# An EdgeConv layer with a segment maximum on one core: final rows from three stretches, the minimum trees behind the second list, and every final addition on VectorE

## The reference, cut to what matters

```python
h = jnp.maximum(_layernorm(x, axis=-1), 0.0)
x_i, x_j = h[dst], h[src]
feat = jnp.concatenate([x_i, x_j - x_i], axis=-1)
msg = feat @ W.T + b                      # W is 128 x 256
out = jax.ops.segment_max(msg, dst, num_segments=6250)
return x + jnp.where(jnp.isfinite(out), out, 0.0)
```

## Time and profile before

| what | value |
|---|---|
| median of 3 runs | 991.62 us (990.52 to 994.15) |
| the profiled execution, its own time | 995.42 us |
| its span | 993.8 us |
| mean granted clock of TensorE | 0.825 of full |
| busy: TensorE / VectorE / ScalarE / GpSimd | 57% / 85% / 58% / 72% |
| DMA | 182.11 MB, mean 183 GB/s |

### The profile page before, as it was taken

How to read it: one execution, slowest core, us unless ns; L and a number is a source line. 1 busy time by engine, 2 the same in 40 slices (tenths; PEclk the granted TensorE clock), 3 DMA queues, 4 the chain that set the end, 5 groups by cost and what they waited for, 6 DMA issues and landing times.

```text
span 993.8 us, 7917 instructions
## 1 busy us (share of the span) xinstructions
PE 564.1 (57%) x2393; PEld 265.1 (27%) x2393; DVE 846.5 (85%) x1237; ACT 577.9 (58%) x255; POOL 713.8 (72%) x644
## 2 busy tenths in 40 slices
PE   2556970000002366766776676788878888676560
PEld 2443640000001122322222232333333333222240
DVE  7899899987785598999989999899999999758573
ACT  3775113000038999597996987496797976844000
POOL 1587878888875677677767676676777677777745
PEclk9898995555555779888878987999999999988875
DMA  8831222212146466656657776998988778754344
GB/s 256 194 97 21 70 71 79 67 50 77 55 145 217 142 208 223 197 174 222 179 170 232 255 253 201 295 296 300 338 302 321 278 239 259 227 186 139 73 79 148
DMA packets 62901, 182.11 MB, mean 183 GB/s; under 512 B 20358, under 2 KB 33140, under 8 KB 56315
## 3 DMA queue, kind: packets, MB, share of 16 engines
q1 hardware_dynamic: 42530, 140.13, 40.7%
q0 software_dynamic: 20144, 40.52, 17.1%
q10 hardware_dynamic: 184, 0.96, 0.3%
HBM read 127.34 MB, written 55.04 MB: 184 GB/s over the span
## 4 chain that ended last, share of the span: by engine, by line
POOL 29%; DVE 26%; issue 19%; DMA 13%; PE 8%; ACT 3%; POOLq 0%; DVEq 0%; SPq 0%; PEldq 0%
POOL rows L669 22%; DVE acc L1191 10%; DMA rows<-near_table,idx 8%; PE ps L787 8%; DVE maxima L1134 5%; POOL ohs L641 4%; POOL hT L648 3%; DVE hT L1141 3%; DMA running_max<-maxima 2%; DVE pos L878 2%; DVE hT L1154 1%; DVE ohs L1179 1%; DMA ohs<-in_dst,begin_i 1%; DMA ohs<-winners 1%; DVE hT L1146 1%
## 5 line engine op out<-in xcount | busy, mean ns | idle before, releaser
L669 POOL DMA_INDIRECT rows<-near_table,idx x527 | 600.3, 1139 | 206.0 <-issue 138.8
L787 PE MATMUL ps<-ohs,near 128*128 128x481 bf16 x1443 | 351.9, 401 | 142.6 <-DVE acc L1191 119.7
L1191 DVE TENSOR_TENSOR acc<-ps,acc 128x1924 f32<-128x1924 f32 x192 | 336.5, 1779 | 21.8 <-PE ps L787 21.6
L1134 DVE SCALAR_TENSOR_TENSOR maxima<-maxima,fresh,rows 128x128 f32<-128x128 f32 x527 | 185.6, 352 | 72.6 <-DMA rows<-near_table,idx 56.2
L787 PEld LDWEIGHTS ps<-ohs,near 128*128 128x128 bf16 x1443 | 143.7, 105 | 350.1 <-DVE acc L1191 125.8
L548 ACT ACTIVATE ohs<-ohs,neg_l 128x6272 bf16<-128x6272 bf16 x25 | 137.9, 5518 | 123.4 <-DMA ohs<-winners 123.4
L541 ACT ACTIVATE hT<-k,off 128x2400 bf16<-128x2400 int16 x49 | 108.9, 2281 | 131.7 <-DVE hT L1146 115.6
L550 ACT ACTIVATE ohs<-ohs 128x6272 bf16<-128x6272 bf16 x25 | 135.8, 5431 | 0.8
L787 PE MATMUL ps<-sorts_mem,near 128*128 128x481 bf16 x468 | 107.8, 385 | 32.7 <-DVE acc L1191 28.6
L773 PE MATMUL ps<-flags,ones 128*128 128x8 f32 x2 | 0.6, 356 | 173.0 <-DVE spare L1167 173.0
L641 POOL DMA_INDIRECT ohs<-src_pad,start_i x49 | 55.0, 1122 | 34.9 <-DVE start_i L891 20.5
(11 more groups left out here) (173 smaller groups left out, 517.4 us busy)
## 6 DMA issues: line engine op xcount, KB each, us to landing
ohs<-winners SPq DMA_DIRECT2D x37, 1568.0 KB, 7.7
running_max<-maxima SPq DMA_DIRECT2D x90, 512.0 KB, 5.1
sorts_mem<-winners SPq DMA_DIRECT2D x12, 1568.0 KB, 8.0
rows<-near_table,idx POOLq DMA_INDIRECT x527
acc<-in_x SPq DMA_DIRECT2D x6, 512.0 KB, 8.2
near_table<-acc SPq DMA_DIRECT2D x12, 256.0 KB, 4.5
base<-in_x SPq DMA_DIRECT2D x1, 2744.0 KB
out_x<-hT SPq DMA_DIRECT2D x12, 224.0 KB
```

What stands on the lines that cost most here:

```text
L669: nc.gpsimd.indirect_dma_start(rows[:, n % (SLOTS * GATHERS), :], None, near_table[:, :], bass.IndirectOffsetOnAxis(idx[:, n:n + 1], 0)).t ...
L787: last = nc.tensor.matmul(bank(4 * (n % 2) + c - UNITS[r][0])[:, 0:CHUNK], near[:, t, part, :], oh[t % OHS][:, at:at + CHUNK], start=part ...
L1134: V.scalar_tensor_tensor(run_at(n + 1), run_at(n), fresh[:, n:n + 1], rows[:, n % (SLOTS * GATHERS), :], ALU.add, ALU.max).then_inc(chain, 1)
L1191: V.tensor_tensor(into, found, into, ALU.max).then_inc(max_done, 1)
```

## The change

Four things change.

1. **Three tables for the final rows** in place of two. HOMES lists (first j, end of j, first step, end of steps): nodes with j below 36 read steps 0 to 415, j from 36 to 43 read steps 232 to 503, j from 44 to 48 read steps 296 to 527. A block of 8 steps is stored in every table whose range holds it, and block 0 in all. That makes 52 + 35 + 30 = 117 stores; the 15 blocks of steps 296 to 415 are stored three times. Groups 9 and 10 (j 36 to 43) are gathered when block 62 is stored, groups 11 and 12 when all is. Five short VectorE instructions more compute the flags and ends (columns 6 to 9 of flags in place of 6 and 7).
2. **The planner's costs.** A gather costs 1.45 us in the checks and the sort, 2.0 us from the words on and 1.28 us in the rounds; each of the nine early groups of finals costs four gathers more; the third round of every fourth tile costs 3.65 us, since VectorE's one-hot stands there.
3. **All additions on VectorE.** L692 and the semaphore final_added are gone; SyncE waits for final_ready alone.
4. **All trees behind the second list.** Trees 0 to 5 stand one after another behind the list and the verdict, ahead of the first dense round; the rest as before. ScalarE's and SyncE's orders follow the same rules as before: load(0) and load(1) stand behind tree 1, distances of batch 4 behind one_hot(0), those of batch 5 behind one_hot(1).

The planner's answer, worked through with both sets of costs, places the chain's steps as follows (steps placed up to and with that piece of VectorE's work):

| behind | before | after |
|---|---|---|
| the third check | 4 | 8 |
| the tile numbers | 28 | 40 |
| the first half of the last stage of compact | 104 | 108 |
| the second list | 112 | 112 |
| tree 1 | 96 | 116 |
| tree 3 | 108 | 120 |
| tree 5, ahead of the first round | 116 | 124 |
| tile 1 (counted from 1) | 120 | 132 |
| tile 10 | 204 | 240 |
| tile 20 | 296 | 360 |
| tile 30 | 376 | 448 |
| tile 40 | 452 | 496 |
| tile 46 | 500 | 528 |
| tile 49 | 524 | 528 |
| behind all rounds | 528 | 528 |

The diff, cut to its core:

```diff
-CUT, CUT_CAP, CUT_LOW = 36, 416, 232
+HOMES = ((0, 36, 0, 416), (36, 44, 232, 504), (44, 49, 296, 528))
+EARLY = HOMES[0][1] // GROUP
...
     for i in range(stages(1)):
         pieces += [("move", 3.8), ("move", 2.7)]
-        if i >= stages(1) - EARLY_TREES:
-            pieces += tree_pieces(trees)
-            trees += 1
     pieces += [("list", 4.0), ("verdict", 3.0)]
...
     for t in range(49):
-        pieces += [("round", 1.85)] * 4
+        pieces += [("round", 1.85)] * 2 + [("round", 3.65 if t % 4 == 0 else 1.85)] + [("round", 1.85)]
...
+    phase, gather = "lists", {"lists": 1.45, "words": 2.0, "round": 1.28}
+    ending = [FINALS_FROM + g * FINALS_EVERY for g in range(EARLY)]
...
+        if name in gather:
+            phase = name
...
-                issue += GATHERS * (1.3 if name == "round" else 1.85)
+                issue += GATHERS * gather[phase]
                 landed += [issue + 3.0] * GATHERS
+                if n + GATHERS in ending:
+                    issue += GATHERS * gather[phase]
...
-    kept = (CUT_CAP, STEPS + CT - CUT_LOW)
+    kept = [cap - low + STEPS * (low > 0) for _, _, low, cap in HOMES]
...
         def homes(i):
 
             n = i * STEPS
-            return [(0, n)] * (n < CUT_CAP) + [(1, 0)] * (n == 0) + [(1, n - CUT_LOW + STEPS)] * (n >= CUT_LOW)
+            return [(h, n - low + STEPS * (low > 0) if n else 0) for h, (_, _, low, cap) in enumerate(HOMES)
+                    if n == 0 or low <= n < cap]
...
             for g, (a, z) in enumerate(spans):
-                if by_pool(g):
-                    sp.wait_ge(final_added, g // 2 + 1)
-                else:
-                    sp.wait_ge(final_ready, g + 1 - min(g // 2 + 1, groups // 2))
+                sp.wait_ge(final_ready, g + 1)
...
             pool.sem_inc(decided, 1)
-            stored(all_blocks)
-            for g in range(early_groups, groups):
+            for g in range(EARLY, groups):
+                for home in HOMES[1:]:
+                    if spans[g][0] == home[0]:
+                        stored(home[3] // STEPS)
                 finals(g)
-            for g, (a, z) in enumerate(spans):
-                if by_pool(g):
-                    pool.wait_ge(joined, g + 1)
-                    nc.gpsimd.tensor_tensor(rowsF[:, a:z, :], rowsF[:, a:z, :], base[:, a:z, :], ALU.add).then_inc(final_added, 1)
...
-                if not by_pool(g):
-                    dve.wait_ge(joined, g + 1)
-                    V.tensor_tensor(rowsF[:, a:z, :], rowsF[:, a:z, :], base[:, a:z, :], ALU.add).then_inc(final_ready, 1)
+                dve.wait_ge(joined, g + 1)
+                V.tensor_tensor(rowsF[:, a:z, :], rowsF[:, a:z, :], base[:, a:z, :], ALU.add).then_inc(final_ready, 1)
```

More of the change, by code:

```diff
@@ L132, in edgeconv @@
     CT = sum(c for _, _, c in PARTS)
-    early_groups = CUT // GROUP
     spans = [(a, min(a + GROUP, tiles)) for a in range(0, tiles, GROUP)]
@@ L141, in edgeconv @@
     first_blocks, all_blocks = first_steps // STEPS, all_steps // STEPS
-    assert D == P and tiles == 49 and rest and 0 < lastj <= CUT and lastp == P - 1
+    assert D == P and tiles == 49 and rest and 0 < lastj <= HOMES[0][1] and lastp == P - 1
     assert chk_p * chk_w == edges and (4 * P - 1) * hop < edges and UNITS[-1][1] * CHUNK >= nodes
     near_table = nc.dram_tensor("near_table", (tiles * P, D), F32, kind="Internal").ap()
-    kept = (CUT_CAP, STEPS + CT - CUT_LOW)
+    kept = [cap - low + STEPS * (low > 0) for _, _, low, cap in HOMES]
     running = [nc.dram_tensor(f"running_max{h}", (P * c, D), F32, kind="Internal").ap() for h, c in enumerate(kept)]
@@ L217, in edgeconv @@
         end_row = sb("end_row", [P, tiles], I32)
-        flags = sb("flags", [P, 8], F32)
-        flag_s = sb("flag_s", [P, 8], F32)
+        flags = sb("flags", [P, 10], F32)
+        flag_s = sb("flag_s", [P, 10], F32)
         disorder = sb("disorder", [P, 1], I32)
@@ L267, in edgeconv @@
         count_ps = bank(7)[:, 256:257]
-        flag_ps = bank(3)[:, 0:8]
+        flag_ps = bank(3)[:, 0:10]
         x_pad_set = sem("x_pad_set")
@@ L333, in edgeconv @@
         final_ready = sem("final_ready")
-        final_added = sem("final_added")
         out_done = sem("out_done")
@@ L344, in by_dve @@
             return t % 4 == 3
-        def by_pool(g):
-            return g % 2 == 0 and g < groups - 1
         def act_count(t):
@@ L646, in finals @@
                 for j in range(a, z):
-                    h = 0 if j < CUT else 1
+                    h = sum(j >= end for _, end, _, _ in HOMES)
                     nc.gpsimd.indirect_dma_start(
@@ L671, in _ @@
                             bass.IndirectOffsetOnAxis(idx[:, n:n + 1], 0)).then_inc(gathered[b % SLOTS], 16)
-                for g in range(early_groups):
+                for g in range(EARLY):
                     if (b + 1) * GATHERS == FINALS_FROM + g * FINALS_EVERY:
@@ L675, in _ @@
                             pool.wait_ge(m_ready, len(batches))
-                            stored(CUT_CAP // STEPS)
+                            stored(HOMES[0][3] // STEPS)
                         finals(g)
@@ L1048, in loser_words @@
                 if h:
[L1049 to L1054, removed]
+                    for i, (begin, end, low, most_steps) in enumerate(HOMES):
+                        of = slice(max(begin, a), end)
+                        if end < z:
+                            then(V.tensor_scalar(flags[:, 6 + i:7 + i], tot[:, end - a:end - a + 1],
+                                                 float(most_steps - first - 1), None, ALU.is_gt))
+                        if low:
+                            then(V.tensor_scalar(flags[0:lastp, 7 + i:8 + i],
+                                                 tot[0:lastp, begin - a:begin - a + 1], float(low - first), None, ALU.is_lt))
+                        then(V.tensor_scalar(end_f[:, of], tot[:, of.start - a + 1:end - a + 1], float(first),
+                                             float(most_steps - 1), ALU.add, ALU.min))
                     settled()
-                    then(V.tensor_scalar(end_f[:, CUT:z], end_f[:, CUT:z], float(STEPS - CUT_LOW), 0.0, ALU.add, ALU.max))
+                    for begin, end, low, _ in HOMES[1:]:
+                        then(V.tensor_scalar(end_f[:, begin:end], end_f[:, begin:end], float(STEPS - low), 0.0, ALU.add, ALU.max))
                 else:
@@ L1064, in loser_words @@
                 settled()
-                for at, end, rows_kept in ((a, CUT, kept[0]), (CUT, z, kept[1])) if h else ((a, z, kept[0]),):
+                for at, end, rows_kept in ([(max(u[0], a), u[1], r) for u, r in zip(HOMES, kept)] if h else [(a, z, kept[0])]):
                     then(V.scalar_tensor_tensor(end_row[:, at:end], part_f[:, 0:1].to_broadcast([P, end - at]),
```

## The result

The changed kernel takes 1009.1 us (median of 4 runs, 1003.2 to 1017.0) where the kernel before takes 992.5 us: ratio 1.0168, 95% interval 1.013 to 1.0205. It is slower, where 981.5 us and a gain were forecast. Its profiled execution took 1005.5 us with a span of 1003.8, so 10.0 us more than the span before; this execution lies 0.4% under its kernel's median and the profiled one of before (995.4 us) 0.3% over its own, which is why the medians stand further apart.

What follows compares the result with a forecast made beforehand. Bounds: GpSimd before the second list, VectorE in the rounds, a chain of single steps at the end. Start 364 + rounds 598.8 + end 21.0 = 983.8 us against 993.8, so 981.5 us beside the median; range 957 to 1002.

Steps and rivals of the forecast that it cites:

- The end: Behind the last round: final rows gathered beside rounds, serial VectorE work left, 21.0 us in place of 40.7, gain 19.7.
- The second list and the start: Ahead of the rounds: list at about 305 us in place of 313, first round at 364, 27 us later.
- The first-list steps placed earlier change nothing: Ahead of the second list: earlier chain steps cost or gain 0 us, since GpSimd bounds this stage.
- The rounds: First to last dense round: 598.8 us in place of 616.3, from 364 to 962.8.
- I take the 29 us as gone: In the rounds: VectorE's 29 us of waits for rows vanish; between 0 and 29 might come back.
- Waits for TensorE: In the last tiles without steps: matmuls and VectorE's rounds nearly equal, 2 us more.
- The stores: In the rounds: 15 blocks stored three times cost 11 us, bounds 0 and 35.
- The bound of 316 GB/s: DMA in the rounds: if 316 GB/s is all there is, eight blocks' 82 us stretch by 16%, 13 us.
- Waits for rows come back: Rival for the rounds, chance 0.15: 1.28 us a gather is best pace, a third of 29 us stays; 991.5 us.
- Slower: the triple stores bind: Rival for the rounds, chance 0.15: three copies land late, 2.3 us for each of 15 blocks; 1005.5 us.
- The test for a wrong forecast: Waits in the rounds: over 15 us for rows would show the forecast wrong.
- the signs of a right one: Whole kernel: first round near 364, last near 963, 21 us behind it, no row wait over 2 behind 850, additions within 0.8.

Runs made afterwards that it cites:

- c4: Changed kernel with a gather in the rounds costing the planner 1.35 us and additions of even groups back on GpSimd; ratio 1.001 to the kernel before.
- c1: Changed kernel with a planner's pace of 1.35 us in the rounds and two tables for the final rows; ratio 0.998 to the kernel before.
- d1: Changed kernel with two tables for the final rows, pace still 1.28 us; ratio 1.009 to the kernel before.
- d2: Kernel before with only the four trees moved behind the second list; ratio 1.016 to the kernel before.
- b2: Changed kernel with one number changed, a gather in the rounds costing the planner 1.35 in place of 1.28 us; ratio 0.992 to the kernel before.
- b3: Changed kernel with pace 1.35 us in the rounds and trees 0 to 3 back among the last four stages of compact; ratio 0.978 to the kernel before.
- c3: Changed kernel with pace 1.35 us in the rounds, tree places and planner's costs ahead of the rounds as before; 965.8 us, ratio 0.971.
- b1: Kernel before with only the three tables for final rows and all additions on VectorE; ratio 0.991 to the kernel before.
- group a: Four variants of the changed kernel, one part undone each, run on a disturbed chip; ratios 1.015, 1.027, 0.987 and 1.025 to the kernel before.
- a2: Changed kernel with two tables for the final rows, run on a disturbed chip; ratio 1.027 to the kernel before.

## Why the prediction was wrong

- **The end: right.** 20.0 us, 21.0 forecast. c4 shows the additions at work (8 us more at the end where GpSimd adds too), and at a pace of 1.35 c1 shows the third table (10 us). At the change's own pace the table did nothing for the end (d1, 20.3 us without it); the early steps did its work.
- **The second list and the start: the numbers right, one step wrong.** 304.1 and 362.1, against 305 and 364. d2 and b2 against b3 confirm what ScalarE's order, which the planner does not know, makes of the moved trees: 15.5 and 15.4 us. But "The first-list steps placed earlier change nothing" is wrong: the planner's new costs ahead of the rounds moved the list back by 11.5 us and the first round by 9.8 (d2), which is the rest of the 25.3 us lost. My sum counted a wait for steps 104 to 107 ahead of the list and took it as given; with the old costs (d2) the list does not wait for them.
- **The rounds: the step that failed is "I take the 29 us as gone".** The gather's pace was taken from the densest 50 us, 39 of them or 1.28 us each, and then only the total was compared (384 gathers and 36 final rows, done by 930). That it fits in total says nothing on the middle: the change asks for 12 steps a tile there, one in 1.29 us, against a gather in 1.41. The lead of 20 rows (I had put it at 24) is down to 4 at 595, and 21.5 us of waits follow. With 1.35 (b2) the waits are 0.9 us and the rounds 597.0, the forecast's 598.8. The row that would have told it is GpSimd's count over a long stretch: 415 gathers and 36 final rows between 313.3 and 951.8, one in 1.42 us, though full buffers hold it up there too. I cited it only for a rival.
- **Waits for TensorE**: 34.8 in place of 25.7 us. TensorE's clock is 0.89 of full over the rounds where it is 0.91 in b2 and before; from 550 to 850 it is 0.88 against 0.93 in b2. Waits for rows do not explain it: b3 has none in its rounds and waits 38.0 us for TensorE, c3 has 8.8 and waits 33.5 at a clock of 0.92. The growth lies in the first, wider round of each tile (15.7 us in the changed kernel and 17.1 in b3, against 4.6 before), in kernels with the new pace; why is open.
- **The stores: sized too high.** 11 us more forecast, 0.3 more measured (2.5 against 2.2 us of waits for stores); in b2, which waits for rows only 0.9 us, they are 10.3, so 8.1 more. The third copy took no more than 5 to 9 us of the rounds here (d1), and none that is clear at a pace of 1.35 (c1). The bound of 316 GB/s was none: the changed kernel moves 324 in its densest 50 us, and b2 350 in the same stretch. The Trainium skill (SBUF — State Buffer, section "SBUF: two separate sides") has 358 GB/s, which put this term at some 2 us. In the changed kernel that was nearer than my 11, in b2 it was not; and slices of 24 us on the pages of b1 and b2 reach 371 and 366 GB/s, a little over the page's figure.
- **The rivals.** "Waits for rows come back" named the mechanism and its reason (1.28 is the best pace, not the mean), but was priced at a third, 10 us, and given 0.15; it also had the old waits behind 850 come back, where new ones came in the middle. "Slower: the triple stores bind" had the side right and the cause wrong: d1, without them, is still 0.9% slower than before. The test for a wrong forecast, waits for rows over 15 us in the rounds, is the one that struck. Of the signs of a right one, those on the start, the end and the additions came true, and no wait for rows behind 850 is over 0.2 us.
- **The sum.** With 621.7 for 598.8 the forecast's own sum would have been 364 + 621.7 + 21.0 = 1006.7, 12.9 us over the span before. The two other terms miss by 3 us together.

## What to carry to other kernels

A planned order is only as good as the slowest pace it counts on: take the producer's pace over a long stretch of the stage where it will be used, not from its best window, and compare running counts of producer and consumer, not totals. Steps placed too early are worse than steps too late here (against 1.35, 1.28 costs 2.6% and 1.40 costs 0.7%), since the consumer stands still with all that is queued behind it, and a lead in buffers only delays the moment. When a change moves one engine's work, read the fixed orders of the others: here 15 us hung on a one-hot that stands ahead of the distances on ScalarE. And when a change has several parts, price each by itself: a right sum for the start hid that 10 of its 25 us came from another part than the one that was blamed.

## What was not expected of the hardware

GpSimd's rate of indirect DMAs hardly depends on DMA traffic: 213 to 220 in 300 us between 252 and 301 GB/s. An undisturbed one takes 0.94 + 0.30 us, so 0.12 to 0.17 us each are lost. The rows above split it: over 0.94 us busy each they hold 13 to 15 us of longer instructions in 300 us, and over 0.30 us between two 12 to 21 us of longer gaps, most of them waits for a batch to land (or, in the kernel before, for a free buffer). Whether a third batch in flight would shorten the gaps, and with them make the pace of 1.28 possible, was not tried. And the chip of group a took 10% longer for the kernel before (1091 against 992 us) and 11% for a2's program (1119 against 1004 us as d1), with waits of VectorE of up to 11 to 15 us for something outside the program.
